# A fused decoder of twelve sublayers on one core: values and denominators of a head in one product, shuffled apart, and projected in two parts

## The reference

```
L0x, L2x, L3a:  p = softmax(scores per head)           # L0x: over the context and, causally, x itself; L3a causal
                out = (p @ v per head) @ W_out
L1a:            s = causal, decaying phi(q) . phi(k)    # linear attention
                out = (s @ v) / (row sums of s + 1e-6) @ Wo, per head, then an RMS norm
L1x:            the same softmax with 16 heads of 64 features
L3x:            mLSTM: exp(log decay matrix) * (q k^T) @ v, per head, normalised
```

## Time and profile before

| | us |
|---|---|
| timed runs: median of 3 (lowest, highest) | 1023.44 (1021.11, 1024.71) |
| profiled execution, span from first to last instruction | 1020.0 |
| TensorE busy in the span | 904.2 (89%), 9368 products and as many weight loads |
| VectorE busy | 539.7 (53%), 1569 instructions |
| ScalarE busy | 450.7 (44%), 923 instructions, 97.5 us of it 76 table loads |
| GpSimd busy | 50.8 (5%) |

### The profile page before, as it was taken

One profiled execution on the slowest core, in us unless ns is written; L12 is line 12 of the kernel. 1 busy time (PEld: TensorE's weight loads), 2 busy tenths in 40 slices (PEclk: granted clock), 3 DMA queues, 4 the chain that ended last, 5 costly groups with the idle time before them and its releaser, 6 DMA issues. The chain is left out here.

```text
span 1020.0 us, 22561 instructions
## 1 busy us (share of the span) xinstructions
PE 904.2 (89%) x9368; PEld 700.2 (69%) x9368; DVE 539.7 (53%) x1569; ACT 450.7 (44%) x923; POOL 50.8 (5%) x71
## 2 busy tenths in 40 slices
PE   7689899999989998997987979989998989899772
PEld 5257768778778785666556757867887868686441
DVE  5733565653265575347636853655325547454345
ACT  2044343453454673574255233244465446433442
POOL 2300000010010000001000000001001000000000
PEclk8799989999999998999999999999999999999965
DMA  9100000401000301103000000040000030000000
GB/s 344 40 2 3 1 1 1 166 2 37 2 19 1 141 3 40 43 12 139 2 12 1 2 1 2 2 166 33 6 1 19 1 140 1 2 1 2 2 1 21
DMA packets 6838, 36.12 MB, mean 35 GB/s; under 512 B 721, under 2 KB 4305, under 8 KB 5458
## 3 DMA queue, kind: packets, MB, share of 16 engines
q1 hardware_dynamic: 6738, 34.68, 9.1%
HBM read 34.15 MB, written 0.52 MB: 34 GB/s over the span
## 5 line engine op out<-in xcount | busy, mean ns | idle before, releaser
L673 PE MATMUL bank<-xT,weights_F 128*128 128x256 f32 x832 | 202.9, 386 | 3.1 <-ACT p L1818 2.6
L673 PEld LDWEIGHTS bank<-xT,weights_F 128*128 128x128 f32 x832 | 152.0, 193 | 26.8 <-issue 4.2
L681 PEld LDWEIGHTS bank<-weights_F,p 128*128 128x128 f32 x1088 | 133.4, 191 | 18.8 <-DVE p L1363 7.2
L681 PE MATMUL bank<-weights_F,p 128*128 128x128 f32 x1088 | 141.3, 278 | 3.7 <-DVE p L1363 3.0
L1743 ACT ACTIVATE p<-bank 128x512 f32<-128x512 f32 x160 | 84.5, 601 | 121.0 <-PE bank L492 120.9
L1683 ACT ACT_TABLE_LOAD x76 | 97.5, 1283 | 12.9 <-DMA weights_con<-in_con 5.9
L1347 DVE SCALAR_TENSOR_TENSOR res<-bank,comb,res 128x128 f32<-128x128 f32 x184 | 55.7, 345 | 74.1 <-PE bank L681 71.6
L1184 DVE TENSOR_REDUCE m_wide<-bank 128x4 f32<-128x512 f32 x96 | 60.3, 684 | 43.4 <-PE bank L780 33.5
L1818 ACT ACTIVATE p<-bank 128x512 f32<-128x512 f32 x72 | 42.5, 597 | 91.6 <-PE bank L673 91.2
L1363 DVE TENSOR_TENSOR p<-p,bank 128x512 f32<-128x512 f32 x72 | 49.3, 685 | 47.5 <-PE bank L673 27.3
L1894 ACT ACTIVATE p<-bank 128x512 f32<-128x512 f32 x64 | 36.6, 598 | 51.3 <-PE bank L673 51.2
(11 more groups left out here) (319 smaller groups left out, 1356.0 us busy)
## 6 DMA issues: line engine op xcount, KB each, us to landing
weights_F<-in_L1f SPq DMA_DIRECT2D x2, 4096.0 KB, 13.8
weights_F<-in_L0f SPq DMA_DIRECT2D x2, 3456.0 KB, 13.4
weights_F<-in_L2f SPq DMA_DIRECT2D x2, 3456.0 KB, 12.1
weights_Y<-in_L1x_kv SPq DMA_DIRECT2D x2, 1024.0 KB, 10.6
weights_Z<-in_L1x SPq DMA_DIRECT2D x2, 1024.0 KB, 12.9
weights_Y<-in_L2a SPq DMA_DIRECT2D x2, 898.0 KB, 4.4
weights_Z<-in_L2x SPq DMA_DIRECT2D x2, 449.0 KB, 3.2
weights_L3m<-in_L3m SPq DMA_DIRECT2D x2, 288.0 KB, 6.1
```

The source lines that it names most:

```text
L673: m = mm(b[:, k * NT:(k + 1) * NT], W[weight][:, f:f + P], s.xT[:], start=True, stop=True)
L681: m = mm(b[:, tk(u)], h[:, tk(u)], w, start=k == 0, stop=k == len(chunks) - 1)
```

## The change

1. `values8` makes values and denominators in one product: `vz` holds for every head 8 value columns, 8 columns of ones and 16 of zeros. Two heads share an output block of 32 rows (8 values, 8 denominators, 8 values, 8 denominators), heads 0 and 1 of a group of four in columns 0 to 127, heads 2 and 3 in columns 128 to 255. The products with `spread` are gone. The floor in L1a is two products ahead of the values.
2. VectorE moves the denominators beside their values (`den_beside`, a `stream_shuffle` of 256 columns from PSUM into `inv`, which lies in the tiles `qs` and `ks`); ScalarE inverts 256 columns there, and `divided` multiplies 256 columns into `attnT`, which has two parts now.
3. `project_split` multiplies the two parts by two weight tiles, `w_split`, into one sum: rows of the output weights shuffled to where the values lie, other rows masked to zero (`split_heads`, once, in the first turn of stream a).
4. L1x's `scores_t` makes all 16 score products of a sample and then the 16 subtractions. L3x's `units` alternates between the two banks, whose weights lie in different 32-row groups.
5. Where TensorE waited for four or more semaphores that one engine raises in order, it waits for the last alone.
6. GpSimd fills the columns of ones (`unit_columns`) at the start and after L1x, which uses the same memory.
7. `TURN_ORDER` is new on every engine; ScalarE's table loads fall from 80 to 72.

```diff
@@ -143,42 +144,52 @@
 TURN_ORDER = {
     "pe":
-        "a1 b1 a2 b1 a2 b1 a2 b3 a1 b1 a1 b1 a1 b2 a1 b2 a3 b1 a2 b1 a1 b2 a1 b1 a1 b2 a1 b1 a1 b1 a2 b1 a6 b1 "
...
+        "a1 b1 a2 b1 a2 b1 a1 b1 a1 b2 a3 b3 a2 b2 a1 b1 a1 b1 a2 b1 a1 b2 a1 b1 a1 b2 a1 b1 a1 b1 a1 b1 a5 b1 "
...
@@ -306,8 +317,9 @@
-            self.attnT = own("attnT", NS, D)
+            self.attnT = own("attnT", NS, 2, T)
             self.qs, self.ks = own("qs", NS, D), own("ks", NS, D)
+            self.inv = [t[:].rearrange("p u d -> p (u d)") for t in (self.qs, self.ks)]
             self.m_wide = own("m_wide", NS, P)
...
@@ -335,7 +347,10 @@
-            return self.vz[:, block, u].rearrange("p g (i w) -> p g i w", w=40)[:, :, :, 0:8]
+            return self.vz[:, block, u].rearrange("p g (i w) -> p g i w", w=32)[:, :, :, 0:8]
+        def unit_columns(self):
+            return self.vz[:].rearrange("p a u g (i w) -> p (a u g i) w", w=32)[:, :, 8:16]
...
@@ -344,6 +359,14 @@
+    SPLIT = ("L0x", "L1a", "L2x", "L3a")
+    w_split = sb("w_split", [P, len(SPLIT), 2, D])
+    def o_parts(st):
+        return [w_split[:, SPLIT.index(st), part] for part in range(2)]
+    PART_ROWS = [[16 * part + 8 * (k // 16) + k % 8 for k in range(32)] for part in range(2)]
+    DEN_ROWS = [16 * (k // 16) + 8 + k % 8 for k in range(32)]
...
@@ -450,13 +473,18 @@
-                def project(st, w, outs=None):
+                def project(st, w, out=None):
                     b = opened("dve", st, "y")
-                    for a in outs or [(st, "o", u) for u in range(NS)]:
-                        pe.wait_ge(*freed(*a))
-                    for u in range(NS):
-                        m = mm(b[:, tk(u)], s.attnT[:, u], w, start=True, stop=True)
+                    pe.wait_ge(*freed(*(out or (st, "o", NS - 1))))
+                    for u in range(NS):
+                        for part, rows in enumerate(w):
+                            m = mm(b[:, tk(u)], s.attnT[:, u, part], rows, start=part == 0, stop=part == len(w) - 1)
                     filled(m, st, "y")
+                def project_split(st):
+                    if turn == 0:
+                        pe.wait_ge(S("split_" + st), 2)
+                    project(st, o_parts(st))
...
@@ -513,18 +541,16 @@
                     b = opened("dve", st, "o", u)
-                    for part in range(2):
-                        cols = slice(part * T, part * T + T)
-                        if part and floor is not None:
-                            mm(b[:, cols], const("tiny16")[32 * u:32 * u + 16], floor, start=True, stop=False)
-                        for n, (blk, probs) in enumerate(blocks):
-                            for i in range(4):
-                                for g_ in range(4):
-                                    w = s.vz[:, blk, u, g_, 32 * i:32 * i + 32] if part == 0 else \
-                                        const("spread")[:, 32 * i:32 * i + 32]
-                                    m = mm(b[rows32(g_), cols], w, probs(g_, i),
-                                           start=n == 0 and i == 0 and not (part and floor is not None),
-                                           stop=n == len(blocks) - 1 and i == 3)
+                    if floor is not None:
+                        for part in range(2):
+                            mm(b[:, part * T:part * T + T], const("tiny16")[32 * u:32 * u + 16, part * T:part * T + T], floor,
+                               start=part == 0, stop=False)
+                    for n, (blk, probs) in enumerate(blocks):
+                        for i in range(4):
+                            part, a = i // 2, 64 * (i // 2) + 16 * (i % 2)
+                            for g_ in range(4):
+                                m = mm(b[rows32(g_), part * T:part * T + T], s.vz[:, blk, u, g_, a:a + 32], probs(g_, i),
+                                       start=n == 0 and i == 0 and floor is None, stop=n == len(blocks) - 1 and i == 3)
                     filled(m, st, "o", u)
...
@@ -546,8 +572,7 @@
                     for u in range(NS):
-                        for i in range(4):
-                            pe.wait_ge(*freed(st, "t", u, 0, i))
+                        pe.wait_ge(*freed(st, "t", u, 0, 3))
                         values8(st, u, [(0, probs_at(4 * u))])
...
@@ -795,17 +815,10 @@
                                 r, c = n % 2, 4 * (n // 2) + j
-                                mm(b[:, j * T:j * T + T], s.k64[rows64(r), c, tk(u)], s.q64[rows64(r), c, tk(u)], start=True, stop=False)
-                            if j == 0:
-                                pe.wait_ge(*freed("L1x", "mT", u))
-                            for n, b in enumerate(banks):
-                                m = less_maximum(u, n, b, j, True)
-                                if j == 3:
-                                    filled(m, "L1x", "t", u, 0, n)
-                    for c in range(0, 8, 2):
-                        pe.wait_ge(*freed("L1x", f"k{c}"))
-                        pe.wait_ge(*freed("L1x", f"q{c}"))
+                                mm(b[:, j * T:j * T + T], s.k64[rows64(r), c, tk(u)], s.q64[rows64(r), c, tk(u)], start=j == 0, stop=False)
+                        less_maxima("L1x", u, banks)
+                    pe.wait_ge(*freed("L1x", "q6"))
                     scores64("L1x", 0, lambda r, c: s.k64[rows64(r), c, tk(0)])
...
@@ -1043,13 +1051,14 @@
                             mm(heads(b[:], 4), ident_bf[:], among(neg_causal_t_bf[:], 4), start=True, stop=False)
-                        for i, b in zip(both, banks):
-                            u, half = i // 2, i % 2
-                            for j in range(4):
+                        for j in range(4):
+                            for i, b in zip(both, banks):
+                                u, half = i // 2, i % 2
                                 h = 4 * half + j
                                 m = mm(b[:, j * T:j * T + T], const("pick")[rows32(u), h:h + 1].to_broadcast([32, P]),
                                        s.gates[rows32(u), 5], start=False, stop=j == 3)
-                            filled(m, "L3x", "D", i)
+                                if j == 3:
+                                    filled(m, "L3x", "D", i)
...
@@ -1201,10 +1210,19 @@
+                def den_beside(st, u):
+                    o.count(dve.stream_shuffle(s.inv[u], bank(st, "o", u)[:, 0:2 * T], DEN_ROWS), sem("den"))
                 def divided(st, u):
-                    b = bank(st, "o", u)
                     dve.wait_ge(*told("inverse"))
-                    o.count(dve.tensor_tensor(s.attnT[:, u], b[:, 0:T], s.res[:, u], ALU.mult), free(st, "o", u))
+                    o.count(dve.tensor_tensor(s.attnT[:, u].rearrange("p a t -> p (a t)"), ring.bank((pair, st, "o", u))[:, 0:2 * T],
+                                              s.inv[u], ALU.mult), free(st, "o", u))
+                def split_heads(st):
+                    done = [o.count(dve.stream_shuffle(to, W[st + "_o"], PART_ROWS[part])) for part, to in enumerate(o_parts(st))]
+                    for part, to in enumerate(o_parts(st)):
+                        dve.wait_ge(*done[part])
+                        o.count(dve.tensor_scalar(to, to, const("values"), None, ALU.mult), S("split_" + st))
...
@@ -1662,6 +1690,11 @@
                             yield from sum_weights()
+                        if pair == 0 and stage in (L0x, L0f):
+                            for st, group in ((("L0x", "L0x"),) if stage is L0x else (("L1a", "L1a"), ("L2x", "small"), ("L3a", "L3a"))):
+                                dve.wait_ge(*weights(group))
+                                split_heads(st)
+                                yield
                         yield from stage()
...
@@ -1748,7 +1781,8 @@
                 def inverses(st, u):
-                    inverse(bank(st, "o", u)[:, T:2 * T], s.res[:, u])
+                    act.wait_ge(*told("den"))
+                    inverse(s.inv[u], s.inv[u])
...
@@ -2090,7 +2125,11 @@
                 def L1x():
-                    yield from rest(lambda: o.count(pool.memset(s.vz[:], 0.0), sem("vz_clean")))
+                    def clean():
+                        link(pool.memset(s.vz[:], 0.0))
+                        o.count(pool.memset(s.unit_columns(), 1.0), sem("vz_clean"))
+                    yield from rest(clean)
                     yield from rest(lambda: add_bias(s.x_tok, "L2a"))
...
```

76 lines of the change are left out of this document (41 added, 35 removed), and 65 rows, old and new, of the table TURN_ORDER.

## The result

The changed kernel takes 1010.4 us (median of 4, 1007.0 to 1012.9), the kernel before 1022.9 beside it (median of 4). The ratio is 0.9876, 95% interval 0.9852 to 0.9900. I had forecast 990, with a range of 969 to 1008: the direction was right, the size far off, and the time lies above the range.

The account below looks back on a forecast made before the run. TensorE, busy 92% of the 867 us middle, was taken as the bound. From 1020.0, minus 42.6 work, plus 7.7 chain and 2 orders, gave 987.1; with 3.4 around the span 990.5, said as 990, range 969 to 1008.

Parts of the forecast that it names:

- Values products: In `values8`, 1280 products with `spread` go at 27.2 ns each: -34.8 us; those left keep their shape.
- L1x: Grouping score products and subtractions cuts a sample from 4.31 to 2.97 us: -10.7 us of TensorE's work.
- Projection: Two parts add 64 instructions of 0.11 us on TensorE in four stages: +7.1 us.
- Rival C: L3x row groups don't run in twos, or L1x grouping brings nothing; 15.8 us stay: 1006 us, chance 0.08.
- the shuffle: VectorE's denominator shuffle of 256 columns from PSUM, ahead of the projection: 0.42 us each, 32 of them.
- The chain: From values products' end to multiplication's end grows 0.85 to 1.92 us; exposed before projections 10.8 instead of 3.1: +7.7 us.
- Rival D: Shuffles at the reciprocal's rate, 1.9 us each, lengthen chains and hold up VectorE's queue: 1030 us, chance 0.05.
- TensorE's own work falls by 42.6: Values, L1x and L3x save 34.8, 10.7 and 5.1 us; floors and projection add 0.9 and 7.1.
- rival E: TensorE's clock falls: 40 us more at 1.2 GHz in attention stages, products 20 to 30 us longer: 1015, chance 0.05.
- new orders, I take +2: New step orders win idle time or lose cover, 0.9 us per values block: -12 to +20 us, taken as +2.
- rival A: Half of TensorE's 42.6 us returns as waits behind maxima, exponentials and shuffles: 1002, or 1008 with longer chain; chance 0.17.
- three signs of being wrong: A shuffle above 1 us, middle idle time above 90 us, or 16 L3x decay products still taking 1.6 us.

Follow-up runs that it names:

- the regroupings alone: Kernel before with only L1x's key-side score products and L3x's decay pairs regrouped, old order tables kept: 1010.1 us, 0.9879.
- filling such waits: Changed kernel with 115 added bfloat16 products, results overwritten, ahead of fourteen of TensorE's waits: 994.6 us, 0.9733 of the kernel before.
- filling its waits: Kernel before with 51 added products, results overwritten, ahead of eight of its own TensorE waits: 1012.7 us, 0.9912.
- the second hundred of them: Changed kernel with the 115 added products plus 102 more, ahead of eleven further waits and four longer at one place: 1000.4 us, 0.9784.

## Why the prediction was wrong, step by step

**Right: TensorE's work.** Values products at 27 ns: the remaining group is unchanged (42.6 us for 1280). L1x: L818 fell from 22.9 to 16.4 us busy, and the regroupings alone took 17.7 us off (15.8). L3x: the decay products fell from 15.1 to 10.4 us (5.1 less forecast). Projection: 6.3 us (7.1). Busy time at the clock of the kernel before was 860.8 us (861.6). Rival C is out.

**Right: the shuffle. The chain in part.** The shuffle takes 0.44 us (0.42), and the wait in front of those projections was 12.6 us (10.8). The Trainium skill (VectorE: DVE Perf Modes, the perf-mode tier table), scaled down, gave an estimate of 0.3 us; the measurement is half as much again. From the shuffle's start to the multiplication's end it is 1.80 us, but the forecast's 1.92 counted from the products' end, and there it holds only where VectorE is free at once: from 535.75 to 539.03 it is 3.28. In at least 9 of the 16 pairs of samples the second shuffle starts more than 1 us after the values products' end, and the median from there to the multiplication's end is 2.9 us. The prediction put this queueing at nothing, up to 5 us, with both engines more than half free in the middle; VectorE was not, with 462.3 of 867 us. That the total wait came near the forecast all the same is partly luck. Rival D, a dear shuffle, is out by its price, yet its mechanism is not: 0.44 us more on each chain cost 17 us.

**Wrong, first: "TensorE's own work falls by 42.6" was taken as time at the clock before.** The work fell, but 11.2 us came back because it ran at 0.96 instead of 0.98 of the clock in the middle. This is rival E, to which I gave 0.05. I had priced a wait at its length. Measured, a wait costs its length and what runs slowly behind it: 0.9 us in the eight products behind 3.4 us of waiting, 1.6 us behind 1.9. The extent was near what E supposed, its price was not: from the mean clocks of 0.934 and 0.952 some 35 us more were spent at the lower level (an estimate, with two levels and both spans), where E had 40, and they cost 11 us of busy time and not 20 to 30. The gain from filling such waits, 15.8 us, is of the size of the miss of 20, but not the same thing: it holds spells that the kernel before had too. I had looked for the low clock at the ends only, where the earlier trace rows showed it; the kernel before had spells in the middle too, as these 10 us show (columns as above), and filling its waits brought 8.8 us.

```profile
380.00:390.00 10.00, 7.43 (x41) 0.78 0.27 105
```

The Trainium skill (TensorE: Matmul & The Clock Gate, Why this matters for your kernels), which names idle gaps between bursts, was right, and my sentence that the trace bore it out only at the ends was wrong.

**Wrong, second: "new orders, I take +2", which also held the lost cover.** Idle time rose by 22 us instead of 9.7. The runs show three parts, each from single traces: the cover that the removed values products gave (9.6 us, back when they are done twice), the shuffles (10.3 us, gone without them) and the regroupings (3.6 us), 23.5 in all. The new tables are not among them. They decide where TensorE waits, at the new x (+13) and in L2a (+5.2), but with the old ones the new code idles 139.4 us, and the old code with the new ones 119.9, only 4.1 more than before. So the cover of 0.9 us a block, which the prediction named and then netted against better orders, was real. This is rival A, with 12 us more idle time than forecast where A had 21. The bound of +20 held. The price of the tables alone (5.2 us) and their worth to the new code (14.7 us) have opposite signs, so no single number for this term was right.

The measured 1010.4 us lies between A's 1008 and E's 1015: both were at work, and the prediction had them exclude each other. None of its three signs of being wrong came up (shuffle above 1 us, more than 90 us idle in the middle, slow decay products), since none of them looked at the clock.

**Not tried:** the merged waits, priced at nothing, were not taken back alone. Nor were the table loads: the trace has 71 instead of 76 (91.1 us instead of 97.5), and no run shows what they are worth.

## What to carry to other kernels

When an engine that is 92% busy gives up work, ask of every piece of it what it covered, and price each wait that appears with what runs behind it: here a third to a half of the cost of a longer chain was TensorE's lower clock after it, and the wait for a place in VectorE's queue belonged to the chain. Look for slow spells in the middle by comparing equal groups of products in the timeline, not by the mean clock. Where a wait can't be shortened, products without use ahead of it can pay; they must end before it does, since the second hundred of them made the kernel slower again (5.8 us).

## What the runs showed of the hardware

- The lower level followed a wait of 1.92 us: 32 products took 5.37 us behind it, and 3.74 us at the same place when TensorE had been kept busy. Behind another of 1.64 us eight products still ran at 1.13 us, and the granted clock fell to 0.50 just after them. The slow spell need not begin at the first product behind the wait.
- Bfloat16 products that do nothing useful kept the clock up for float32 products behind them: 1.00 instead of 0.50 at the projection shown, 1.16 us for its eight products instead of 2.05.
- Changes of shape cost: 256 score products of 64 rows take 22.9 us when they alternate in fours with products of 32 rows, and 16.4 us in unbroken rows.
- A shuffle of 128x256 float32 from a PSUM bank takes 0.44 us and is preceded by a 0.01 us load of its mask.
- Executions of one kernel differ with the clock that they were granted: the change without shuffles took 987.2 us at a mean of 0.953 and 1000.9 us at 0.930; with products in its waits, 989.9 to 1002.3 us.
